# A new order of work on all five engines in the group steps of a gated attention and expert kernel

## The reference

```python
x  = x + tanh(g_xattn[0]) * xattn(layernorm(x), ctx)   # 16 heads of 64
x  = x + tanh(g_ffn[0])   * moe(layernorm(x))          # 14 experts, the best one per token

def xattn(x, context):
    q, k, v = layer_norm(x) @ Wq, layer_norm(context) @ Wk, layer_norm(context) @ Wv
    return (softmax(q @ k.T / 8) @ v) @ Wo             # per sequence and head

def moe(x):
    logits = x @ router_w
    a      = argmax(logits)
    return softmax(logits)[a] * (gelu(x @ w1[a] + b1[a]) @ w2[a] + b2[a])
```

## Time and profile before

| | us |
|---|---|
| median of 3 runs | 804.44 |
| lowest and highest | 803.19, 805.55 |
| span of the profiled execution | 800.6 |
| TensorE matmul busy | 752.9 (94%) |
| VectorE busy | 584.8 (73%) |
| ScalarE busy | 568.7 (71%) |
| GpSimd busy | 477.2 (60%) |

### The profile page before, as it was taken

One profiled execution on the slowest core, in us unless ns is written; L12 is line 12 of the kernel. 1 busy time (PEld: TensorE's weight loads), 2 busy tenths in 40 slices (PEclk: granted clock), 3 DMA queues, 4 the chain that ended last, 5 costly groups with the idle time before them and its releaser, 6 DMA issues. The chain is left out here.

```text
span 800.6 us, 34985 instructions
## 1 busy us (share of the span) xinstructions
PE 752.9 (94%) x12820; PEld 698.4 (87%) x12821; DVE 584.8 (73%) x1592; ACT 568.7 (71%) x1171; POOL 477.2 (60%) x1032
## 2 busy tenths in 40 slices
PE   5799999999999999999999999999999987888884
PEld 5689999999999999999999999999999977788884
DVE  5357777777777777777777777877777765477774
ACT  3677878777777777777777777777787743266663
POOL 3454466666666666666666666666666442277776
PEclk8999999999999999999999999999999997799997
DMA  5850011111111101111111111111100000355540
GB/s 127 238 142 20 20 35 34 32 31 31 31 31 31 31 31 31 31 31 31 31 31 31 31 31 38 31 31 33 37 23 23 22 22 28 106 172 150 150 135 28
DMA packets 50002, 43.56 MB, mean 54 GB/s; under 512 B 14488, under 2 KB 45498, under 8 KB 49946
## 3 DMA queue, kind: packets, MB, share of 16 engines
q1 hardware_dynamic: 43466, 30.14, 13.6%
q0 software_dynamic: 5536, 12.66, 4.5%
q10 hardware_dynamic: 944, 0.01, 0.1%
HBM read 28.15 MB, written 15.48 MB: 55 GB/s over the span
## 5 line engine op out<-in xcount | busy, mean ns | idle before, releaser
L453 POOL TENSOR_TENSOR probs<-probs,row_inv 128x1024 f32<-128x1024 f32 x64 | 122.0, 1906 | 46.9 <-DVE row_inv L1148 46.1
L578 ACT ACTIVATE KT<-psJ 128x512 f32<-128x512 f32 x128 | 76.2, 595 | 51.1 <-PE psJ L778 48.2
L1143 DVE TENSOR_REDUCE row_sum<-probs 128x16 f32<-128x1024 f32 x64 | 77.7, 1215 | 39.5 <-ACT probs L629 39.5
L623 ACT ACTIVATE PTs<-psT 128x512 f32<-128x512 f32 x128 | 75.9, 593 | 33.4 <-PE psT L872 33.4
L1156 DVE TENSOR_TENSOR OT_l<-psO,OT_h 128x1024 fp32r<-128x1024 f32 x64 | 78.1, 1221 | 24.7 <-ACT OT_h L616 24.6
L578 ACT ACTIVATE V<-psJ 128x512 f32<-128x512 f32 x128 | 73.2, 598 | 25.9 <-PE psJ L778 22.7
L1128 DVE TENSOR_REDUCE row_max<-psS 128x16 f32<-128x1024 f32 x64 | 75.6, 1181 | 12.3 <-PE psS L835 12.3
L629 ACT ACTIVATE probs<-probs 128x1024 f32<-128x1024 f32 x64 | 67.8, 1059 | 23.0 <-DVE probs L1135 22.9
L872 PE MATMUL psT<-ident,probs 128*128 128x128 f32 x512 | 78.8, 276 | 3.8 <-ACT PTs L623 2.6
L776 PE MATMUL psJ<-CT_h,Wk_h 96*128 96x256 f32 x256 | 77.9, 304 | 4.1 <-ACT QT L578 3.7
L489 POOL DMA_INDIRECT rows_by_expert<-rows,place_i x64 | 64.3, 1005 | 25.6 <-issue 25.6
(11 more groups left out here) (229 smaller groups left out, 2198.4 us busy)
## 6 DMA issues: line engine op xcount, KB each, us to landing
V<-rows_by_expert SPq DMA_DIRECT2D x40, 129.0 KB
QT<-rows_by_expert SPq DMA_DIRECT2D x37, 129.0 KB, 2.2
x_in<-in_x_dram SPq DMA_DIRECT2D x32, 128.0 KB, 2.1
x_res<-in_x_dram SPq DMA_DIRECT2D x32, 128.0 KB, 2.1
c_in<-in_ctx_dram SPq DMA_DIRECT2D x32, 96.0 KB, 2.2
rows_by_expert<-pad_row SPq DMA_DIRECT2D x1, 1806.0 KB, 12.0
w_sb<-in_L_ffn_w_dram SPq DMA_DIRECT2D x1, 1792.0 KB, 8.3
rows_by_expert<-rows,place_i POOLq DMA_INDIRECT x64, 2.6
```

The costliest lines, as they stand in the source:

```text
L453: pool.tensor_tensor(pr, pr, row_inv[:, p.k % 2, :].unsqueeze(2).to_broadcast([P, 16, SEQ]), ALU.mult).then_inc(s_norm, 1)
L578: act.activation(dst, psJ[n % 2][:, :], ACT.Copy).then_inc(s_jobev, 1)
L623: act.activation(PTs[:, (p.k - 1) % 2, half, :], psT[:, :], ACT.Copy).then_inc(s_ptev, 1)
L1143: dve.tensor_reduce(row_sum[:, :], pr, AX.X, ALU.add).then_inc(s_sum, 1)
```

## The change

Every engine's `step` gets a new order.

- TensorE: jobs 2 to 5 stand together, and jobs 6 to 9 (6 and 7 move from the even to the odd step); `router` moves up behind `post_a`, `rank` into the odd step between `scores` and `value_sums`, `prep` behind `probs_T(0)`, `post_b` behind `out_proj`. The runs are 0-1, 2-5, 6-9 and 10-11 with `out_proj`.
- Banks: `router` writes to `psS`, `post_b` to `psO`; `psM` keeps `prep`, `out_proj`, `post_a` and `rank`. The list `misc` is replaced by waits written out in each helper.
- ScalarE follows with its copies; `norm_in` moves to the end of the even step, `norm_x2` and `norm_T` behind `expo` and `attn_out`.
- VectorE: `values_low` comes before `residual` in the even step, `places` at the head of the odd step, `scores_sub` and `values_low` before `weight` and `prep`.
- GpSimd: in both steps `normalise` changes place with what stood around it.

The diff, cut to its core (the last steps, written out by hand, and the routing behind them change in the same manner):

```diff
@@ GpSimd @@
                 if p.odd:
                     split_in(p)
+                    normalise(p)
                     send(p)
+                else:
                     normalise(p)
-                else:
                     roots(p)
-                    normalise(p)
@@ ScalarE @@
                 elif p.odd:
-                    job(p, 8)
-                    norm_x2(p)
-                    job(p, 9)
                     values_high(p)
+                    for n in range(6, 10):
+                        job(p, n)
                     probs_out(p, 0)
-                    norm_T(p)
                     job(p, 10)
                     job(p, 11)
                     expo(p)
+                    norm_x2(p)
+                    attn_out(p)
+                    norm_T(p)
                     probs_out(p, 1)
-                    attn_out(p)
                 else:
-                    if not (p.fixed and p.s == 0):
-                        norm_in(p)
                     values_high(p)
...
                     job(p, 4)
                     job(p, 5)
+                    probs_out(p, 1)
                     route_exp(p)
-                    job(p, 6)
-                    probs_out(p, 1)
-                    job(p, 7)
+                    norm_in(p)
@@ TensorE: waits @@
             def scores(p):
...
                     pe.wait_ge(s_jobev, 12 * p.g + 10)
+                elif p.group(3) is not None:
+                    pe.wait_ge(s_dl, p.g - 2)
             def value_sums(p):
...
+                if not p.odd and p.group(3) is not None and not (p.fixed and p.s >= PAIRS):
+                    pe.wait_ge(s_n2T, p.g - 2)
             def out_proj(p):
...
-                misc_free()
+                if p.group(-2) is not None:
+                    pe.wait_ge(s_xf, 2 * (p.g + 3))
@@ TensorE: steps @@
                 elif p.odd:
                     scores(p)
+                    rank(p)
+                    value_sums(p)
+                    for n in range(6, 10):
+                        job(p, n)
+                    probs_T(p, 0)
                     prep(p)
-                    job(p, 8)
-                    job(p, 9)
-                    value_sums(p)
-                    probs_T(p, 0)
                     job(p, 10)
-                    post_b(p)
                     job(p, 11)
...
                     out_proj(p)
+                    post_b(p)
                     probs_T(p, 1)
                 else:
                     scores(p)
...
                     job(p, 0)
                     job(p, 1)
                     post_a(p)
+                    router(p)
                     probs_T(p, 0)
-                    job(p, 2)
-                    job(p, 3)
-                    router(p)
-                    job(p, 4)
-                    job(p, 5)
+                    for n in range(2, 6):
+                        job(p, n)
                     probs_T(p, 1)
-                    rank(p)
-                    job(p, 6)
-                    job(p, 7)
@@ VectorE @@
                 if p.odd:
+                    places(p)
                     scores_max(p)
+                    scores_sub(p)
+                    values_low(p)
                     weight(p)
                     prep(p)
-                    values_low(p)
-                    scores_sub(p)
                     sums(p)
                 else:
...
+                    values_low(p)
                     residual(p)
                     means_x2(p)
                     route(p)
-                    places(p)
-                    values_low(p)
                     sums(p)
```

More of the change, by code:

```diff
@@ L683, in step @@
                     job(p, 1)
-                    if p.fixed and p.s == 0:
-                        norm_in(p)
                     expo(p)
@@ L783, in prep @@
                     return
-                misc_free()
+                if p.fixed and p.g < 2:
+                    if p.g > -2:
+                        pe.wait_ge(s_xf, 2 * (p.g + 2))
+                elif p.fixed and p.g < 3:
+                    pe.wait_ge(s_x2, p.g - 1)
+                else:
+                    pe.wait_ge(s_ranked, p.g - 2)
                 pe.wait_ge(s_z, 4 * (p.g + 3))
@@ L908, in post_b, with router @@
                 last.then_inc(s_postb, 1)
-                misc[b] = (s_n2T, p.g - 1)
-            def router(p, b=0):
+            def router(p, out=psS):
                 if p.group(3) is None:
                     return
-                misc_free(b)
+                if not (p.fixed and p.s >= PAIRS):
+                    pe.wait_ge(s_sub, p.s + 1)
                 pe.wait_ge(s_n2T, p.g - 2)
                 for t in range(2):
-                    last = pe.matmul(banks[b][:, E * t:E * t + E], n2T[:, P * t:P * t + P], rw_sb[:, :], start=True, stop=True)
+                    last = pe.matmul(out[:, E * t:E * t + E], n2T[:, P * t:P * t + P], rw_sb[:, :], start=True, stop=True)
@@ L918, in router, with rank @@
                 last.then_inc(s_logit, 1)
-                misc[b] = (s_dl, p.g - 2)
-            def rank(p, b=0):
+            def rank(p, out=psM):
                 if p.group(3) is None:
                     return
-                misc_free(b)
                 pe.wait_ge(s_hot, p.g - 2)
-                pe.matmul(banks[b][:, 0:E], before[:, :], onehot[:, 0, :], start=True, stop=True)
-                pe.matmul(banks[b][:, E:2 * E], ones_b[:, :], onehot[:, 0, :], start=True, stop=False)
-                pe.matmul(banks[b][:, E:2 * E], before[:, :], onehot[:, 1, :], start=False, stop=True)
-                pe.matmul(banks[b][:, 2 * E:3 * E], ones_b[:, :], onehot[:, 0, :], start=True, stop=False)
-                pe.matmul(banks[b][:, 2 * E:3 * E], ones_b[:, :], onehot[:, 1, :], start=False, stop=True).then_inc(s_rank, 1)
-                misc[b] = (s_ranked, p.g - 2)
+                r0, r1, r2, r3 = (E * i for i in range(4))
+                pe.matmul(out[:, r0:r1], before[:, :], onehot[:, 0, :], start=True, stop=True)
+                pe.matmul(out[:, r1:r2], ones_b[:, :], onehot[:, 0, :], start=True, stop=False)
+                pe.matmul(out[:, r1:r2], before[:, :], onehot[:, 1, :], start=False, stop=True)
+                pe.matmul(out[:, r2:r3], ones_b[:, :], onehot[:, 0, :], start=True, stop=False)
+                pe.matmul(out[:, r2:r3], ones_b[:, :], onehot[:, 1, :], start=False, stop=True).then_inc(s_rank, 1)
@@ L1054, in _ @@
             probs_T(D64, 1)
-            rank(D64, 1)
+            rank(D64, psJ[1])
             value_sums(D65)
@@ L1058, in _ @@
             out_proj(D65)
-            post_b(D65, 1)
+            pe.wait_ge(s_sub, PAIRS)
+            post_b(D65, psS)
             post_a(D66)
-            router(D66, 1)
+            router(D66, psS)
             spin(6, psJ[0])
-            rank(D66, 1)
+            rank(D66, psS)
             pe.wait_ge(s_bias, 32)
@@ L1363, in _ @@
             last_roots(D66)
-            route(D66, psJ[1])
-            places(D66, psJ[1])
+            route(D66, psS)
+            places(D66, psS)
             weight(D67)
-            route(D68)
-            places(D68)
+            route(D68, psJ[1])
+            places(D68, psJ[1])
             weight(D69)
```

53 lines of the change are left out of this document (22 added, 31 removed).

## The result

| | before | after |
|---|---|---|
| median of the runs | 804.5 us (803.2 to 805.6, 4 runs) | 847.9 us (847.3 to 850.1, 4 runs) |
| span of the profiled execution | 800.6 us | 845.6 us |
| granted clock of TensorE, mean, same execution | 0.967 | 0.969 |

The ratio is 1.056, with a 95% interval of 1.053 to 1.058: slower by 43 us. The prediction was 823.0 us, with a range of 811 to 834. The direction was right, and the size was less than half of what came.

What follows compares the result with a forecast made beforehand. A closed loop over GpSimd, the row write and VectorE, 20.24 us a group against 19.64 before, was to become the bound: 26 x 0.60 = 15.6, plus 3.0 for the tail, on 804.4 gives 823.0 us, range 811 to 834.

Steps and rivals of the forecast that it cites:

- TensorE bounds the kernel before: In the loop before the change, TensorE was taken as the bound, 19.64 us a group, 99.94 of 100 us busy.
- TensorE's own sum of 19.8 us: TensorE's time per group in the new order: 19.64 - 0.33 + 0.48 = 19.8 us.
- the inner waits: Inside the two runs of four jobs, TensorE waits for ScalarE's copies out of the banks: 0.48 us a group.
- the entries: Seven runs of projections become four on TensorE, saving three entries of 0.11 us, 0.33 us a group.
- The closed loop of 20.24 us: Chain through both normalises, roots, split_in, send, landing, residual, route and sums sets the period: 20.24 us a group.
- Nothing in it can be overlapped, so its length is a lower bound.: Claim that the steps of the GpSimd, row write and VectorE loop run strictly in turn, so the period is at least 20.24 us.
- The rival of the port: VectorE's prep, two operations of 0.53 us, blocks GpSimd's roots: loop 1.06 us longer, 850 us; chance 0.03.
- The landing: Time from send's second row write until it lands and releases residual, taken as 2.5 us in the loop.
- The input loads that SP issues after norm_in are needed only in the next group.: Claim that moving norm_in to the end of ScalarE's even step delays no needed load; no cost was counted.
- The signs: Profile marks named beforehand; wrong if residual does not wait for the write, or GpSimd idles before split_in.
- 26 groups: Of 32 groups, 26 (24 to 28) were counted as paying 0.60 us each, 15.6 us.
- the tail: In the last odd step send comes behind normalise, so residual waits for the write: 3.0 us once, 1 to 4.

Runs made afterwards that it cites:

- kernel 3: Kernel 1 with GpSimd's send put back ahead of normalise in the odd step; 816.7 us.
- kernel 4: Kernel 3 with ScalarE's norm_in put back at the front of the even step; 813.4 us.
- kernel 5: Kernel 4 with GpSimd's roots put back ahead of normalise in the even step; 815.2 us.
- kernel 1: The changed kernel with the sums of places written to PSUM, so the place multiplication reads PSUM and SBUF; 829.4 us, and 828.6 in another set.
- kernel 2: The changed kernel with VectorE's places moved behind values_low in the odd step, operands left in SBUF; 829.9 us.
- kernel 6: The changed kernel with only ScalarE's norm_in put back at the front of the even step; 854.5 us.

## Why the prediction was right and wrong

Going by its own steps:

- **TensorE bounds the kernel before.** Right.
- **TensorE's own sum of 19.8 us.** 20.04 was measured (kernels 3, 4, 5). The jobs' part came as said, 0.15 more, with both terms too large: 0.39 instead of 0.48 for the inner waits, about 0.24 instead of 0.33 for the entries. The 0.23 around the small blocks was missing.
- **The closed loop of 20.24 us.** Right as a loop without holds: 20.28 in one turn of kernel 1, 20.30 over 22 groups, and residual waited 2 us as said.
- **"Nothing in it can be overlapped, so its length is a lower bound."** Right, and it was then used as if it were the length itself. This is the step that failed: split_in was put directly behind roots, with no wait for prep, and the hold of VectorE by GpSimd's normalise was put at nothing in the sum. The runs showed a wait of 0.64 to 0.68 us a group there and a period of 21.04 to 21.07; without the hold (kernels 1 and 2) it is 20.3, and 18 to 19 us are gone. Joint by joint, the changed kernel's group above against the sum:

| part of the loop | predicted | measured |
|---|---|---|
| normalise even to the end of roots | 6.72 | 337.99 - 331.27 = 6.72 |
| wait of split_in for prep | 0 | 0.64 |
| split_in | 2.66 | 341.28 - 338.63 = 2.65 |
| normalise odd to the second write | 4.35 | 345.49 - 341.28 = 4.21 |
| landing to residual | 2.55 | 348.31 - 345.49 = 2.82 |
| residual to sums | 2.39 | 350.75 - 348.31 = 2.44 |
| sums to normalise even | 1.57 | 352.33 - 350.75 = 1.58 |
| sum | 20.24 | 21.06 |

  The 0.64 is VectorE's branch beside roots: places, the maximum, the subtraction, values_low, weight, prep. It was never summed. From the start of normalise to the end of prep it takes 5.57 us in kernel 1 (404.80 to 410.37) and ends before roots, which need 6.72; with the hold it takes 7.20 (331.27 to 338.47). So summing the branch alone would not have found the wait: the hold had to be known too. Of its 1.6 us the slack of the branch takes 1.15.
- **The rival of the port.** The mechanism was right and its place was wrong. It was put at roots beside prep, and it is at places beside normalise; it was given 0.03 because of one pair of rows. prep reads PSUM there and could not show it. That its time, 850, lies near the 847.9 measured is luck: it charged 1.06 us a group to roots, which were not held (normalise and roots took 6.72 us together, as summed). A row of the kernel before did show the hold: weight's last step, 128x2 elements, in ns as minimum, median, maximum.

```profile
L1223 DVE TENSOR_SCALAR rows<-inv,tanhs x32: 228/610/614, 99.9 to 680.8; 128x2 f32<-128x2 f32 x32
```
```profile
316.24 0.61 DVE L1223 TENSOR_SCALAR rows<-inv,tanhs 128x2 f32<-128x2 f32 x1
```

  The second row is its run in the group of the earlier trace rows, from 316.24 to 316.85, beside the normalise that ended at 316.82. In the changed kernel, away from normalise, it takes 228 every time. Such a ratio of median to minimum for the same shape was the thing to ask about.
- **The landing.** 2.5 was the least of the rows; 2.7 is the median after. With 2.6 or 2.7 the sum is 20.34 to 20.44, and kernel 1 says 20.30. In the group above the landing is the second largest part of the miss, 0.27.
- **"The input loads that SP issues after norm_in are needed only in the next group."** Wrong at the start, where they cost some 3 us that the sum put at nothing. In the middle the late norm_in even helps the closed loop, by 7 us (kernel 6), and the traces suggest that it does so because the loads keep clear of the row writes.
- **The signs.** It wanted to be wrong if GpSimd idles before split_in, "then TensorE's own sum decides". GpSimd did idle there, but the loop decided all the same, only longer.
- **26 groups, and the tail.** The last waiting residual of the changed kernel is at 702.51, after 2.94 us of waiting; 3.0 was predicted.

What the 44 us are made of, by the steps between kernels: kernel before to kernel 4, 10.0 (TensorE's new order, 26 x 0.38); 4 to 3, 3.3 (norm_in, across two sets); 3 to 1, 11.9 (the loop: 26 x 0.25 = 6.5 from the period, the rest in the first and last groups, not split further); 1 to the changed kernel, 847.4 - 828.6 = 18.8 (the hold, 26 x 0.75 = 19.5 by the periods). The sum is 44.0, where the prediction had 18.6. Its loop of 15.6, which includes TensorE's part, and its tail of 3.0 stand against 10.0 + 11.9 = 21.9 here. The rest is the hold and the start. None of the kernels beats the kernel before.

## What to carry to other kernels

Where a change closes a loop over several engines, sum every branch between two joints, take the longer one, and note how much slack the shorter has: here it was 1.2 us, and a hold of 1.6 us used it up. When an instruction moves beside another engine's long one, ask for the spread of its duration in the trace, not the mean, and look where its operands lie: one operand in PSUM was worth 18 us here. And orders of engines come in packages: a helper that is moved back on one engine alone cost 110 us and more, because the helper on another engine that uses or frees the same buffer had moved with it. Where an engine stands still for some us in every group, look at the granted clock behind the gap as well.

## What the hardware did that was not expected

- A 28-element multiplication on VectorE took 1.84 us instead of 0.18 beside a GpSimd multiplication of 1.90 us, both reading SBUF. The same instruction with one input and the output in PSUM, at the same place, took 0.19.
- A row write landed in 3.2 us instead of 2.6 in the kernel in which 224 KB of input loads were issued between its two halves.
- On two of the chips TensorE paused in the 64-wide matmuls of every group's even step, some 2.1 us a group; on the others the same kernel did not. The stage behind the row writes, the same in all kernels, took some 42 us longer there.
